# Cross attention, two layers: bulk loads issued from ScalarE's queue in small pieces, transposed scores 16 groups behind, row maxima transposed ahead of the value product and split one maximum sooner

## The reference, cut to what matters

```
q = x @ Wq + bq                       # 32 heads of 8 features
k = context @ Wk + bk                 # 8 key heads, each serves 4 query heads
v = context @ Wv + bv
scores = q k^T / sqrt(8) + mask       # 32 x 128 x 128
attn   = softmax(scores)
y      = (attn @ v) @ Wo + bo + x
x      = layernorm(y) * gamma + beta  # input of the second layer
```

## Time and profile before

| what | value |
|---|---|
| median of three runs | 337.89 us |
| the profiled execution, its own time | 340.19 us |
| its span in the trace | 338.3 us |
| PE busy | 292.6 us (86%) |
| DVE busy | 271.5 us (80%) |
| ACT busy | 209.1 us (62%) |
| POOL busy | 194.0 us (57%) |
| mean granted TensorE clock | 0.93 of full speed |
| DMA, mean | 131 GB/s, 44.40 MB |

### The profile page before, as it was taken

The page is one execution under the profiler, slowest core; times in us unless marked ns, Lnnn a source line. Parts: engine busy times, 40 slices in busy tenths (PEclk is TensorE's granted clock), DMA queues, the critical chain, the costliest instruction groups (busy, mean ns, idle before and its releaser), DMA issues.

```text
span 338.3 us, 8301 instructions
## 1 busy us (share of the span) xinstructions
PE 292.6 (86%) x2890; PEld 196.8 (58%) x2890; DVE 271.5 (80%) x625; ACT 209.1 (62%) x500; POOL 194.0 (57%) x335
## 2 busy tenths in 40 slices
PE   7466399599998999999899999999999999888851
PEld 4366276277666776776566666666666666554320
DVE  4426449489988998999899999999999999999441
ACT  3601257277766777777677777777777777656540
POOL 6123305366766776776656666666666666444464
PEclk9756769699999999999999999999999999999795
DMA  7584766714674446344634434444444444420000
GB/s 280 168 237 114 213 182 179 212 31 122 182 242 135 118 124 183 100 125 131 178 101 112 115 109 120 126 121 137 132 119 121 137 141 130 122 64 18 20 16 31
DMA packets 34555, 44.40 MB, mean 131 GB/s; under 512 B 11857, under 2 KB 28241, under 8 KB 31697
## 3 DMA queue, kind: packets, MB, share of 16 engines
q1 hardware_dynamic: 33952, 43.27, 44.7%
q10 hardware_dynamic: 560, 0.59, 0.5%
HBM read 33.10 MB, written 9.96 MB: 127 GB/s over the span
## 4 chain that ended last, share of the span: by engine, by line
PE 37%; DVE 35%; DMA 14%; issue 9%; SPq 2%; ACT 1%; POOL 1%; POOLq 0%; ACTq 0%; DVEq 0%
DVE row_max L460 18%; DMA q_stack<-max_parts 9%; PE misc_bank L663 8%; PE s_bank L567 7%; PE t_bank L587 7%; PE oT_bank L647 7%; DVE o_sb L481 4%; DMA q_scratch<-q_parts 4%; PE qkv_bank L613 3%; DVE z L499 3%; DVE attnT L492 3%; DVE max_parts L468 2%; DVE recip L487 2%; PE qkv_bank L619 2%; PE qkv_bank L623 1%
## 5 line engine op out<-in xcount | busy, mean ns | idle before, releaser
L460 DVE TENSOR_REDUCE row_max<-s_bank 128x4 f32<-128x512 f32 x256 | 168.8, 678 | 35.9 <-PE s_bank L567 35.0
L365 ACT ACTIVATE probs<-t_bank 128x512 f32<-128x512 f32 x256 | 148.0, 601 | 77.8 <-PE t_bank L587 77.4
L587 PE MATMUL t_bank<-q_stack,k_stack 75*128 75x512 bf16 x256 | 99.8, 393 | 20.4 <-DMA q_stack<-max_parts 12.6
L567 PE MATMUL s_bank<-k_stack,q_stack 72*128 72x128 bf16 x1024 | 102.3, 225 | 8.2 <-DMA k_stack<-k_scratch 7.4
L567 PEld LDWEIGHTS s_bank<-k_stack,q_stack 72*128 72x128 bf16 x1024 | 76.2, 101 | 53.1 <-issue 18.5
L307 POOL TENSOR_TENSOR rstd<-var_eps,minus_half 128x1 f32<-128x1 f32 x32 | 17.6, 548 | 56.0 <-DVE var_eps L507 56.0
L316 POOL TENSOR_TENSOR attn<-o_sb,recip 128x256 f32<-128x256 f32 x32 | 20.0, 625 | 40.0 <-DVE recip L487 39.7
L587 PEld LDWEIGHTS t_bank<-q_stack,k_stack 75*128 75x128 bf16 x256 | 25.0, 99 | 28.4 <-ACT probs L365 13.1
L663 PE MATMUL misc_bank<-wo_sb,attnT 128*128 128x256 f32 x128 | 36.0, 405 | 5.7 <-DVE attnT L492 5.7
L190 POOL TENSOR_TENSOR q_rest<-qT,q_parts 128x256 f32<-128x256 f32 x30 | 20.1, 669 | 34.4 <-ACT q_parts L374 34.4
L374 ACT ACTIVATE qT<-qkv_bank,bq_scaled 128x128 f32<-128x128 f32 x60 | 22.1, 369 | 22.6 <-PE qkv_bank L623 20.8
(11 more groups left out here) (76 smaller groups left out, 359.2 us busy)
## 6 DMA issues: line engine op xcount, KB each, us to landing
q_stack<-q_scratch SPq DMA_DIRECT2D x32, 576.0 KB
q_scratch<-q_parts SPq DMA_DIRECT2D x32, 192.0 KB, 6.2
k_stack<-k_scratch SPq DMA_DIRECT2D x32, 144.0 KB
in_sb<-inputs SPq DMA_DIRECT2D x3, 1024.0 KB, 7.9
x_sb<-x SPq DMA_DIRECT2D x4, 512.0 KB, 5.5
result<-y SPq DMA_DIRECT2D x16, 128.0 KB, 1.7
k_scratch<-k_parts SPq DMA_DIRECT2D x48, 32.0 KB, 3.5
mask_sb<-mask SPq DMA_DIRECT2D x1, 1024.0 KB, 7.2
```

The lines of the kernel that those rows point to most:

```text
L365: nc.scalar.activation(probs[:, u % 2, kv], t_bank[kv % 2][:], ACT.Exp).then_inc(exp_done, 1)
L460: nc.vector.tensor_reduce(row_max[:, u % 2, GROUP * kv:GROUP * (kv + 1)], s_bank[(KV * u + kv) % S_BANKS][:].rearrange("p (g s) -> p g s", ...
L567: mm = nc.tensor.matmul(to[:, g * S:(g + 1) * S], q_stack[0:TERM_ROWS, slot, GROUP * kv + g], k_stack[0:TERM_ROWS, slot, kv], start=(g == ...
L587: mm = nc.tensor.matmul(t_bank[kv % 2][:], k_stack[0:STACK_ROWS, slot, kv], q_stack[0:STACK_ROWS, slot, GROUP * kv:GROUP * (kv + 1)], star ...
```

## The change

Five edits:

1. `LAG` goes from 15 to 16. Head 0 of unit t-2 is now computed transposed in turn 0 of phase t, and head 7 in turn 7.
2. On PE, `probs_v(t-3, 1)` moves from after turn 0 to after `transpose_max`, which follows turn 1 as before; `probs_v(t-2, 0)` moves from after turn 4 to after turn 5.
3. On DVE, `max_rows(t-1)` moves from after maximum 2 and the reciprocal to right after maximum 1, ahead of `flip_o`.
4. All bulk loads of the phases leave SP's queue. ACT issues them at the end of its phase (`load_later`): inputs one sequence at a time (256 KB) for phases -2 to 10, x in groups of two (256 KB) instead of four, the rows and Wo one layer at a time (384 KB and 256 KB), Wq of layer 1 in phase 9 instead of 3. At the start SP loads one sequence of inputs instead of two.
5. The waits follow the smaller pieces: one semaphore a sequence of inputs, one a layer of rows and of Wo.

```diff
-LAG = 15
+LAG = 16
-X_GROUP = 4
+X_GROUP = 2
-INPUT_GROUPS = ((0, 1), (1, 2), (2, 4), (4, 8), (8, 12), (12, 16))
...
-        def load_inputs(engine, group):
-            first, end = INPUT_GROUPS[group]
-            engine.dma_start(in_sb[:, first:end].rearrange("p b a k l -> p (b a k l)"),
-                             inputs[:, first:end].rearrange("p b a k l -> p (b a k l)")).then_inc(inputs_loaded[group], 16)
+        def load_inputs(engine, b):
+            engine.dma_start(in_sb[:, b].rearrange("p a k l -> p (a k l)"),
+                             inputs[:, b].rearrange("p a k l -> p (a k l)")).then_inc(inputs_loaded[b], 16)
...
-                if t in (-2, 2, 6):
-                    load_inputs(sp, 3 + (t + 2) // 4)
-                if t == 0:
-                    sp.dma_start(rows_sb[:], rows_d[:, 0:3 * D].partition_broadcast(P)).then_inc(rows_loaded, 16)
-                if t > 0 and t % X_GROUP == 1 and t < BATCH:
-                    sp.dma_start(x_sb[:, t - 1:t - 1 + X_GROUP],
-                                 x[t - 1:t - 1 + X_GROUP].rearrange("b l d -> l b d")).then_inc(x_loaded[t // X_GROUP], 16)
-                if t == 1:
-                    sp.dma_start(wo_sb[:].rearrange("p a k n -> p (a k n)"), w_o).then_inc(wo_loaded, 16)
-                if t == 3:
-                    sp.dma_start(wq1_sb[:], w_q1).then_inc(wq1_loaded, 16)
...
+            def load_later(t):
+
+                if t + 5 < BATCH:
+                    load_inputs(act, t + 5)
+                if t in (0, 8):
+                    layer = t // 8
+                    act.dma_start(rows_sb[:, layer],
+                                  rows_d[layer:layer + 1, 0:3 * D].partition_broadcast(P)).then_inc(rows_loaded[layer], 16)
+                if 0 < t < BATCH and t % X_GROUP == 1:
+                    act.dma_start(x_sb[:, t - 1:t - 1 + X_GROUP],
+                                  x[t - 1:t - 1 + X_GROUP].rearrange("b l d -> l b d")).then_inc(x_loaded[t // X_GROUP], 16)
+                if t in (2, 10):
+                    layer = t // 10
+                    act.dma_start(wo_sb[:, layer].rearrange("p k n -> p (k n)"),
+                                  w_o[:, layer * LEAD:(layer + 1) * LEAD]).then_inc(wo_loaded[layer], 16)
+                if t == 9:
+                    act.dma_start(wq1_sb[:], w_q1).then_inc(wq1_loaded, 16)
...
                     copy_yT(t - 4)
+                if -AHEAD < t:
+                    load_later(t)
...
                 maximum(t, 1)
+                if live(t - 1):
+                    max_rows(t - 1)
                 if live(t - 3):
                     flip_o(t - 3)
                 maximum(t, 2)
                 if live(t - 3):
                     reciprocal(t - 3)
-                if live(t - 1):
-                    max_rows(t - 1)
                 maximum(t, 3)
...
                 scores(t, 0, masked)
                 scoresT(g, masked)
-                if live(t - 3):
-                    probs_v(t - 3, 1)
                 scores(t, 1, masked)
                 scoresT(g + 1, masked)
                 if live(t - 1):
                     transpose_max(t - 1)
+                if live(t - 3):
+                    probs_v(t - 3, 1)
                 scores(t, 2, masked)
...
                 scoresT(g + 4, masked)
+                scores(t, 5, masked)
+                scoresT(g + 5, masked)
                 if live(t - 2):
                     probs_v(t - 2, 0)
-                scores(t, 5, masked)
-                scoresT(g + 5, masked)
```

More of the change, by code:

```diff
@@ L51, in reads_before @@
     return 6 * min(u, BATCH) + 4 * max(u - BATCH, 0)
-def input_group(b):
-    return next(n for n, (first, end) in enumerate(INPUT_GROUPS) if first <= b < end)
 def need(engine, sem, count):
@@ L142, in cross_attention @@
         bv_loaded = sem("bv_loaded")
-        rows_loaded = sem("rows_loaded")
-        wo_loaded = sem("wo_loaded")
+        rows_loaded = sems("rows_loaded", LAYERS)
+        wo_loaded = sems("wo_loaded", LAYERS)
         masks_loaded = sem("masks_loaded")
         x_loaded = sems("x_loaded", BATCH // X_GROUP)
-        inputs_loaded = sems("inputs_loaded", len(INPUT_GROUPS))
+        inputs_loaded = sems("inputs_loaded", BATCH)
         stacks_loaded = sems("stacks_loaded", RING)
@@ L331, in add_bo @@
                 layer, b = place(u)
-                if u == 0:
-                    pool.wait_ge(rows_loaded, 16)
+                if b == 0:
+                    pool.wait_ge(rows_loaded[layer], 16)
                 if layer == 0 and b % X_GROUP == 0:
@@ L607, in project @@
                 need(pe, yT_copied, min(u - AHEAD - 4, BATCH))
-                if layer == 0 and b == INPUT_GROUPS[input_group(b)][0]:
-                    pe.wait_ge(inputs_loaded[input_group(b)], 16)
+                if layer == 0:
+                    pe.wait_ge(inputs_loaded[b], 16)
                 w = (lead_sb if layer == 0 else wq1_sb)[:, 0:LEAD].rearrange("p (k n) -> p k n", k=KT)
@@ L655, in project_out @@
                 pe.wait_ge(flip_step, FLIP_STEPS * (u + 1))
-                if u == 0:
-                    pe.wait_ge(wo_loaded, 16)
+                if u % BATCH == 0:
+                    pe.wait_ge(wo_loaded[layer], 16)
                 if live(t - 1):
```

## The result

The changed kernel took 341.4 us, median of four runs (340.82 to 342.28), against 337.92 for the kernel before in the same round. The ratio is 1.0111, 95% interval [1.008, 1.0143]. The forecast was 333, faster; in this comparison it came out 1.1% slower. (Some executions of either kernel take over 1.5% longer than its fastest; they count in the medians, and the ratios leave them out.) Run again later beside other kernels, on a chip where both spread over 5 to 7 us, the ratio was 0.9987 [0.9939, 1.0034]. So the sign of the small loss rests on the first comparison alone, four runs of each kernel; that the gain did not come rests on both.

The account below looks back on a forecast made before the run. PE bounds layer 0; in layer 1 PE and DVE wait for each other. Start -7.4, phases 5 to 12 +0.2, next three -0.4, layer 1 +1.6, tail +1.0: -5.0, so 333 us; range 329 to 341, likeliest case 330 to 336.5.

Parts of the forecast that it names:

- Part 6: Bulk loads beside the maxima DMA, in another queue: a stall of 0.2 us a phase, bounds 0 and 0.5.
- the 9.01: Layer 0 period in us with PE's new order, turn 5 waiting for exponential 3; 8.74 before, +0.27.
- Part 5: LAG 16 issues stacks later, ahead of the maxima DMA: maxima land about M' + 9.2, wanted at 9.47, slack 0.3 us.
- rival C: DMA queue becomes layer 0's bound, at late maxima or stacks: stall 0.7 us a phase, 342 us in all; chance 0.20.
- the sign that the prediction gave for rival C: PE idle before turn 0 on the maxima or the stacks in most phases of layer 0.
- The sign for its own forecast: No chain piece of a maxima DMA over 4 us after 50 us.
- the 2.75: Estimated undisturbed time in us of the maxima DMA, under the bound of 3.2.
- The upper bound of part 6: Stall of 0.5 us a phase from bulk loads, expected if DMAs of all issuers share the same 16 engines.
- Part 7: The start, to M of phase 5: 67.8 us instead of 75.2, gain 7.4, bounds 1.8 and 9.7.
- Parts 1 and 2: PE's new order, scoresT of turn 5 waiting for exponential 3: +0.27 us a phase in layer 0, +0.10 in layer 1.
- Part 3: DVE's order, three instructions moved ahead of the flip with nothing added: taken as 0.
- Part 8: The tail: head 7 of unit 31 computed in turn 7, behind project_out of unit 30: +1.0 us (0 to 1.6).

Follow-up runs that it names:

- e6: The changed kernel with all bulk pieces issued by ACT at the end of phase -1; ratio 1.0316.
- e2: The kernel before with only the bulk loads as changed (pieces, ACT's queue), LAG 15 and old orders; ratio 0.9996.
- e9: The kernel before with bulk loads cut into the changed kernel's pieces and phases, but issued by SP; ratio 0.9998.
- e5: The changed kernel with its pieces issued by SP behind the parts of unit t+3, instead of by ACT; ratio 1.0328.
- e4: The changed kernel with the maxima's DMA issued by ACT behind exponential 3, in ACT's queue instead of SP's; ratio 1.0012.
- e8: The changed kernel with four filler matmuls of zeros on PE in turn 2 of phases 29 to 31; 340.01 us, ratio 1.0051.
- e10: The kernel before with its own large bulk groups, sizes and phases, issued by ACT instead of SP; ratio 0.9971.
- e1: The changed kernel with LAG back at 15, all else as changed; ratio 1.0032.
- e12: e1 with the first half of the value product back after turn 4; 337.83 us, ratio 0.9924.
- e13: e5 with LAG back at 15, PE's and DVE's orders as changed; ratio 1.0023.
- e14: e12 with the pieces issued by ACT up to phase 2 and by SP from phase 3; 334.69 us, ratio 0.9854.
- e11: The kernel before with ACT's pieces to phase 2, then groups of four in SP's queue; ratio 1.0123.
- e7: e2 with the inputs' piece issued between max_first and the norm, the others behind exponential 2; ratio 1.0005.

## Why the prediction was wrong

**Part 6, the stall of 0.2 us a phase, is the step that failed.** The pieces in flight cost 0.68 us a phase on top of the 9.01: measured on the changed kernel 9.69, forecast 9.21, +3.8 us over eight phases. Without pieces in flight the same kernel has phases of 9.04 to 9.05 (e6). Part 6 asked whether the maxima are late and not whether the next stacks are. In SP's queue each unit's parts land about 8.1 us after the stacks ahead of them were issued, and the stacks behind wait for them. Part 5 worked out this very number and used it for the maxima only. Against a phase of 8.74 that leaves 0.6 us. With LAG 15 pieces in ACT's queue use it up and more: the parts land 9.3 to 9.8 us behind, and a phase takes 9.75 us with the old orders (e2), 9.27 with the same pieces in SP's queue (e9).

For the changed kernel itself, with LAG 16, the account is weaker. The round trip is stretched there too (8.7 to 10.1 us), but with the pieces back in SP's queue it is not, and the phase stays at 9.73 (e5). So with LAG 16 it is the pieces in flight that cost, and not their queue. Which of the late maxima and the late stacks sets the phase was not separated, and the old large groups with LAG 16 were not tried. What PE waits for is the maxima, six times in eight phases (4.3 us), the sign that the prediction gave for rival C. The sign for its own forecast, no DMA of the maxima over 4 us after 50 us, did not come (5.2 to 6.5).

Part 6 also had its price wrong. It took 512 KB ahead of the maxima at 4.40 - 2.75 us and scaled by the bytes. No run shows the 2.75, nor the 0.9 of part 5; the traces give only the bound of 3.2. And in the kernel before the same DMA behind 1 MB took hardly more:

```profile
99.23 4.49 DMA q_stack<-max_parts
```

It counted the pieces short as well: 256 KB in even phases, 512 in odd ones. With the rows, Wo and Wq of layer 1, phases 8, 9 and 10 issue 640, 768 and 512 KB, and the phases in which these run take 10.16, 9.89 and 10.30 us, the other five 9.43 in the mean.

Rival C named this outcome and almost its price (9.71 a phase), but I gave it 0.20; it also named the stacks as one of two places. Its total of 342 came near the measured one in part by luck: it took the start's gain at 3 us, which was 7, and had nothing for the clock. The Trainium skill's rule that all issuers share 16 engines (page "DMA: Bandwidth & Descriptors", section "Issuing engines are not separate DMA queues") fits: in e4 the maxima, moved to the other queue, still took 4.76 us in layer 1. The upper bound of part 6 (0.5 a phase) was nearer than the 0.2, and still under the 0.68.

**The clock at the end was missing.** The last phases of layer 1 project no unit. In the changed kernel the granted clock falls twice there, 2 x 1.5 = 3.0 us, and with filler it does not (e8). The kernel before has the same lighter phases at full clock in both its traces, with waits as long; what tips the clock is open. The prediction asked about the clock in the start only.

**Part 7, the start: right, and step by step.** The maxima of unit 0 land at 39.5 us (forecast 39.0), phases 3 and 4 begin at 49.1 and 58.0 (48.9, 57.7), the maxima of unit 2 are 1.1 us late (1.3), and the clock does not fall after it. M stands at 68.11 and 69.04, forecast 67.8; the transpose of unit 4 at 69.33, "near 69". The gain goes with the clock: the ten traces in which it stays up between 58 and 72 us have M at 68.0 to 72.0, the eight in which it falls there 72.2 to 75.2 (e6, with all pieces ahead, left out). How much of it the queue brings and how much the pieces is not separated (e9, e10).

**Parts 1 and 2, PE's order: right.** 8.58 in layer 1, to the hundredth; 9.04 to 9.05 in layer 0 where nothing hides it (e6), for 9.01. With the round trip stretched it is mostly covered: with the order half undone layer 0 goes from 9.86 to 9.81 only (e1, e12).

**Part 3, DVE's order at 0:** e12 shows -0.05 us a phase for it together with the second half's move; they were not separated.

**Part 5, LAG's other side:** in layer 0 +0.28 us a phase with the pieces in SP's queue (e5, e13), -0.17 with them in ACT's (changed kernel, e1). In layer 1 the maxima are late in most phases and it costs nothing, since turn 5 waits for ACT afterwards.

**Part 8, the tail:** forecast +1.0, measured -0.6 on the first pair of traces and +1.0 on the second. Before's own tail moved by 1.6 between them: in the first the clock stands at 0.50 from 315.1 to 318.5 us, in the second it is at 1.00 there. Against the trace without that fall the forecast is right.

In sum against the first trace: start -7.1, layer 0 +4.0 (+0.2 forecast), phases 13 to 15 -0.1, layer 1 +4.7 (+1.6), tail -0.6: +0.9 of span, forecast -5.0.

## What to carry to other kernels

When a transfer moves to another queue, work out the period of each loop that runs through the first queue (store, wait, load), not only the latency of the one transfer that was late; its slack is what the moved bytes use up (0.4 to 0.5 us a phase here with LAG 15). Where an exponential frees the buffer of a matmul, keep long work between the two on TensorE: 0.10 us a phase in layer 1 and 0.27 in layer 0 could be read off the old trace. And measure each part of a change by itself: without LAG 16 and the first half's move, and with the later pieces in SP's queue, the rest was worth 1.5% (e14).

## What the runs showed of the hardware that I had not expected

After a wait of PE of 2.14 us the granted clock fell, to a mean of 0.59 over the next 4 us (e10). After waits of 3.4 and 2.2 us (e11) and of 2.0 (phase 15 of before's second trace) it fell too. But one of 2.12 us, before 63.26 us in e10 itself, left it at 1.00, and so did those of 1.3 to 1.5 us in layer 0 (e2, e9, e12); in e7 it fell after one of 1.6. So the length of the last wait alone doesn't tell. At the end of layer 1 it fell in nine of 18 traces without a wait over 1.1 us, in the changed kernel with PE busy for 7.25 of 8.36 us in the stretch ahead, and four extra matmuls a phase (8.0 to 8.1 of 8.45) kept it up (e8). And a DMA of 24 KB alone in its queue took 4.76 us beside the other queue's stacks, where the kernel before had it in at most 3.2.
